# Layer 0 of a fused two-layer transformer: two pairs embedded together, every step of the pipeline placed anew

## What is computed

```python
x0 = concat([cls, patches(x) @ w_tok + b]) + pos        # 37 rows of 256 per image
h  = concat([x0, txt])                                  # 32 sequences of 69 rows of 256
xn = layernorm(h);  A = causal softmax(Q K / 4)         # 16 heads of 16
h  = h + (sum over heads of A V) @ WO + 16*bO           # heads are summed before WO
x2 = layernorm(h);  expert = argmax(softmax(x2 @ Wr))   # 8 experts, one per token
h  = h + max_prob * (relu(x2 @ W1[e]) @ W2[e])
# layer 1: attention with 16 heads, then a ternary-weight feed-forward net with a convolution
```

## Time and profile before

| | us |
|---|---|
| median of 3 runs | 916.31 (915.96 to 918.7) |
| the profiled execution's own time | 916.32 |
| its span, first to last instruction | 914.5 |
| TensorE busy | 784.6 (86%) |
| VectorE busy | 600.3 (66%) |
| ScalarE busy | 438.3 (48%) |
| GpSimd busy | 382.4 (42%) |

### The profile page before, as it was taken

How to read it: one execution, slowest core, us unless ns; L and a number is a source line. 1 busy time by engine, 2 the same in 40 slices (tenths; PEclk the granted TensorE clock), 3 DMA queues, 4 the chain that set the end, 5 groups by cost and what they waited for, 6 DMA issues and landing times.

```text
span 914.5 us, 20695 instructions
## 1 busy us (share of the span) xinstructions
PE 784.6 (86%) x7145; PEld 690.6 (76%) x7145; DVE 600.3 (66%) x1444; ACT 438.3 (48%) x1048; POOL 382.4 (42%) x516
## 2 busy tenths in 40 slices
PE   2799999999999987259999399999999999999743
PEld 2799898999898886136766289898888888888532
DVE  0246666666666665542222035899999999999893
ACT  0234444344344442212222156777887778776552
POOL 0234444444444442232221376666656666543100
PEclk9999999999999998579999699999999999999655
DMA  5324831100000023112221100000000000000000
GB/s 149 92 63 192 199 59 47 19 12 8 8 8 8 11 49 107 41 31 70 64 68 43 30 8 14 8 10 18 14 14 15 14 14 18 16 8 8 10 10 12
DMA packets 23981, 36.41 MB, mean 40 GB/s; under 512 B 10037, under 2 KB 21210, under 8 KB 23114
## 3 DMA queue, kind: packets, MB, share of 16 engines
q1 hardware_dynamic: 14474, 26.20, 10.6%
q0 software_dynamic: 5808, 5.63, 2.8%
q10 hardware_dynamic: 3600, 3.28, 1.1%
HBM read 27.21 MB, written 7.88 MB: 38 GB/s over the span
## 4 chain that ended last, share of the span: by engine, by line
PE 42%; DVE 33%; issue 13%; DMA 4%; ACT 4%; POOL 2%; SPq 1%; DVEq 0%; ACTq 0%; POOLq 0%
PE bank_c L1471 5%; PE bank_h L1434 4%; PE bank_b L1462 3%; PE bank_e L1589 3%; DVE stats L902 3%; PE bank_c L1605 2%; PE bank_f L1589 2%; PE bank_d L1605 2%; DVE diff L1110 2%; DVE w L1167 2%; DVE w L1136 2%; DVE rowmax L1102 2%; DVE diff L896 2%; DVE w L1142 2%; DVE zmax L1161 2%
## 5 line engine op out<-in xcount | busy, mean ns | idle before, releaser
L457 POOL TENSOR_TENSOR qbd<-qt,consts_f 128x560 f32<-128x560 f32 x128 | 163.4, 1283 | 196.6 <-PE bank_e L1406 75.5
L465 POOL TENSOR_TENSOR veps<-mv,consts_f 69x2 f32<-69x2 f32 x64 | 12.4, 194 | 141.9 <-DVE mv L906 104.6
L584 ACT ACTIVATE pt<-bank_g 69x448 f32<-69x448 f32 x64 | 34.9, 545 | 70.3 <-PE bank_h L1416 70.3
L1471 PE MATMUL bank_c<-patches,w_tok 128*128 128x74 f32 x384 | 52.4, 292 | 14.9 <-DMA br<-in_br 14.9
L579 ACT ACTIVATE prob<-diff 112x345 f32<-112x345 f32 x64 | 31.4, 491 | 65.4 <-DVE diff L896 65.4
L1471 PEld LDWEIGHTS bank_c<-patches,w_tok 128*128 128x128 f32 x384 | 50.2, 209 | 14.9 <-issue 14.9
L735 ACT ACTIVATE w<-w,conv 128x138 f32<-128x138 f32 x128 | 54.8, 492 | 9.4 <-DVE w L1119 9.4
L503 POOL DMA_INDIRECT diff<-expert_rows,tile_tokens x25 | 25.1, 1004 | 80.4 <-PE bank_a L1581 54.4
L1780 PE MATMUL bank_b<-f,w 128*69 128x256 bf16 x256 | 37.4, 309 | 15.4 <-ACT w L748 14.5
L484 POOL DMA_INDIRECT expert_lists<-token_no,slot_i x32 | 38.5, 1202 | 22.1 <-issue 14.6
L1434 PE MATMUL bank_h<-values,pt 69*69 69x68 f32 x512 | 39.3, 232 | 8.9 <-ACT pt L584 6.8
(11 more groups left out here) (239 smaller groups left out, 2335.4 us busy)
## 6 DMA issues: line engine op xcount, KB each, us to landing
w<-in_w SPq DMA_DIRECT2D x2, 4096.0 KB, 16.3
patches<-in_patches SPq DMA_DIRECT2D x16, 222.0 KB, 2.7
expert_results<-prob ACTq DMA_DIRECT2D x25, 128.0 KB, 1.9
expert_rows<-x SPq DMA_DIRECT2D x16, 138.0 KB
out<-h SPq DMA_DIRECT2D x16, 138.0 KB
f_raw<-in_f SPq DMA_DIRECT2D x2, 1024.0 KB, 8.5
patches<-in_b SPq DMA_DIRECT2D x1, 2048.0 KB, 10.8
wqkv<-in_wqkv SPq DMA_DIRECT2D x2, 768.0 KB
```

What stands on the lines that cost most here:

```text
L457: pool.tensor_tensor(qbd[u % 2][:], q.broadcast_to([128, NG, HPB, QG]), head_mask.unsqueeze(1).unsqueeze(3).broadcast_to([128, NG, HPB, QG ...
L1471: ins = mm(banks["c"][:, m * 2 * IMG:(m + 1) * 2 * IMG], w_tok[:, c, m * 128:(m + 1) * 128], patch_v[:, bass.ds(s, 1), c, :].rearrange("p ...
```

## The change

Two pairs are embedded by one set of products: `embed(i)` makes half i % 2 of the double pair i // 2 with 148 columns, once per step, where before two halves of 74 columns were made per step. `et` has two buffers, the transposes (`turn_embedded`) are still one pair at a time. The first two pairs' patches are loaded ahead of the attention weights, and the loops of SP are unrolled.

The whole order of layer 0 is replaced on all four engines. Every operation becomes a function of its own (most were already so for layer 1, and those are moved up and shared); the functions `softmax_shift`, `moments`, `attend_out` and `move_pt` are split. The pipeline is deeper: lags reach 6 on TensorE and POOL, 5 on DVE and ACT, where they reached 4.

```diff
-    with sp.Fori(1, PAIRS) as n:
+    load_pair(1)                      # ahead of the attention weights
+    for n in range(2, PAIRS):
...
@@ gpsimd
+            def list_tokens(p):
+                pool.wait_ge(slots_made, p + 1)
+                wait(pool, rows_listed, 32 * p)
+                ... two indirect DMAs as before
             def body(s):
-                spread_queries of pair s-2, units 2 and 3
-                inverse_deviation 1 of s-3
-                the two indirect DMAs of s-4
-                inverse_deviation 0 of s
-                spread_queries of pair s-1, units 0 and 1
+                list_tokens(s - 6)
+                deviation2(s - 4)
+                deviation1(s - 1)
+                spread_query(s - 2, 0), (s - 2, 1), (s - 2, 2), (s - 2, 3)
@@ scalar
             def body(s):
+                exp_scores(s-4, 0), exp_scores(s-4, 1), move_pt_g(s-4, 0), move_pt_h(s-4, 0)
+                move_pt_h(s-4, 1), exp_scores(s-4, 2), move_pt_g(s-4, 1), norm2_routed(s-5)
+                move_pt_g(s-4, 2), move_pt_h(s-4, 2), move_x2(s-5), exp_scores(s-4, 3)
+                move_q(s-3), move_pt_g(s-4, 3), move_pt_h(s-4, 3), move_k(s-3)
+                norm1(s-2), move_embedded(s), move_xt(s-2), move_ot(s-4)
@@ vector
             def body(s):
-                softmax_shift(s-2, 0), (s-2, 1), add and moments of s-3, take_slots(s-4)
-                softmax_shift(s-2, 2), add_base and moments of s, softmax_shift(s-2, 3)
-                attend_out(s-2, 0), choose(s-3), attend_out(s-2, 1), move_v(s-1)
+                shift_scores(s-3, 2), row_max(s-3, 3), add_base(s-1), take_slots(s-5)
+                stats_embedded(s-1), shift_scores(s-3, 3), variance1(s-1)
+                row_sums(s-3, 0), norm_heads_summed(s-3, 0), choose(s-4), sum_heads(s-3, 0)
+                row_sums(s-3, 1), norm_heads_summed(s-3, 1), sum_heads(s-3, 1)
+                row_max(s-2, 0), shift_scores(s-2, 0), move_v(s-2)
+                row_max(s-2, 1), shift_scores(s-2, 1), row_max(s-2, 2)
+                add_projected_heads(s-3), stats2(s-3), variance2(s-3)
@@ tensor
+            def embed(i):
+                d, m = i // 2, i % 2
+                pe.wait_ge(patches_in, 16 * (2 * d + 2))
+                bank_is_free("c", "embed", i)
+                for c in range(FC):
+                    ins = mm(banks["c"][:, 0:4 * IMG], w_tok[:, c, m * 128:(m + 1) * 128],
+                             patch_v[:, 2 * d:2 * d + 2, c, :], start=c == 0, stop=c == FC - 1)
             def body(s):
+                scores(s-4, 3), turn_embedded(s-2), turn_p(s-4, 1), rank(s-6), queries(s-3)
+                attend(s-4, 0), turn_p(s-4, 2), attend(s-4, 1), turn_x2(s-5), attend(s-4, 2)
+                logits(s-5), turn_p(s-4, 3), values(s-3), keys(s-3), attend(s-4, 3), embed(s)
+                scores(s-3, 0), turn_x(s-2), scores(s-3, 1), turn_sums(s-4), scores(s-3, 2)
+                project_sums(s-4), turn_p(s-3, 0)
-            steps(pe, PAIRS, LAGS, body)
+            steps(pe, PAIRS, 6, body)
...
```

More of the change, by code:

```diff
@@ L687, in _ @@
+            steps(act, PAIRS, 5, body)
             act.wait_ge(ffn_w_in, 32)
@@ new lines, in bank_is_free, with bank_is_moved, turn_x, queries @@
+            def bank_is_free(bank, stage, p):
+                wait(pe, BK[bank], read_before(order, bank, stage, p))
+            def bank_is_moved(bank, stage, p):
+                pe.wait_ge(BK[bank], read_after(order, bank, stage, p))
+            def turn_x(p):
+                pe.wait_ge(S["x_made"], 2 * p + 2)
+                bank_is_free("a", "turn_x", p)
+                turn_rows("a", xn).then_inc(S["x_turned"], 1)
+            def queries(p):
+                bank_is_moved("a", "turn_x", p)
+                bank_is_free("c", "q", p)
+                query_or_key("c", 0).then_inc(S["q_made"], 1)
@@ new lines, in keys, with query_or_key @@
+            def keys(p):
+                bank_is_moved("a", "turn_x", p)
+                bank_is_free("a", "k", p)
+                query_or_key("a", 1).then_inc(S["k_made"], 1)
+            def query_or_key(bank, kind):
+                for m in range(KC):
+                    for c in range(KC):
+                        ins = mm(banks[bank][:, m * 2 * TP:(m + 1) * 2 * TP],
+                                 wqkv[:, c, kind * D + m * 128:kind * D + (m + 1) * 128],
+                                 xt[:, c, :, :].rearrange("p b t -> p (b t)"), start=c == 0, stop=c == KC - 1)
+                return ins
@@ L1395, in scores, with values @@
+            def values(p):
+                bank_is_moved("a", "turn_x", p)
+                bank_is_free("b", "v", p)
+                for b in range(2):
+                    for c in range(KC):
+                        ins = mm(banks["b"][0:T, b * D:(b + 1) * D], xt[:, c, b, 0:T], wqkv[:, c, 2 * D:3 * D],
+                                 start=c == 0, stop=c == KC - 1)
+                ins.then_inc(S["v_made"], 1)
+            def scores(p, u):
                 b, m, bank = u // 2, u % 2, "ef"[u % 2]
@@ L1396, in scores @@
                 pe.wait_ge(S["qbd_made"], UNITS * p + u + 1)
[L1397 to L1401 removed]
+                bank_is_moved("a", "k", p)
+                bank_is_free(bank, f"scores{u}", p)
                 sc = banks[bank][0:SR, :]
@@ new lines, in body @@
+                if live(s, 6, PAIRS):
+                    rank(s - 6)
+                if live(s, 3, PAIRS):
+                    queries(s - 3)
+                if live(s, 4, PAIRS):
+                    attend(s - 4, 0)
+                    turn_p(s - 4, 2)
+                    attend(s - 4, 1)
+                if live(s, 5, PAIRS):
+                    turn_x2(s - 5)
+                if live(s, 4, PAIRS):
+                    attend(s - 4, 2)
+                if live(s, 5, PAIRS):
+                    logits(s - 5)
@@ L1484, in body @@
+                if live(s, 4, PAIRS):
+                    turn_p(s - 4, 3)
+                if live(s, 3, PAIRS):
+                    values(s - 3)
+                    keys(s - 3)
+                if live(s, 4, PAIRS):
+                    attend(s - 4, 3)
                 if live(s, 0, PAIRS):
-                    embed(s, 0)
+                    embed(s)
+                if live(s, 3, PAIRS):
+                    scores(s - 3, 0)
                 if live(s, 2, PAIRS):
-                    scores(S, BK, order, s, s - 2, 1)
+                    turn_x(s - 2)
```

660 lines of the change are left out of this document (263 added, 397 removed).

## The result

The changed kernel takes 890.3 us, the median of four runs (885.9 to 894.16), beside 916.13 for the kernel before (914.09 to 918.7): a ratio of 0.9715, with 0.9658 to 0.9772 as its 95% interval. The profiled execution is the one of 892.59 us, span 890.8, so 23.7 us less than the 914.5 of before.

A forecast was written before the change was run, and what follows sets the result against it. Layer 0 was taken as bound by TensorE's own work. The steps (-8.4 us), the start (+1) and the end (-1) summed to -8.4 us on 916.32, so 908 us, with a range of 892 to 922.

The forecast's parts named there:

- 15 steps: Layer 0 from the first scores of pair 0 to those of pair 15: 296.4 us against 304.8, 8.4 less.
- projection to the last scatter landed: Layer 0 behind pair 15's projection: statistics and scatters of pairs 14 and 15 as before, so no change.
- What bounds it: Layer 0 is bound by TensorE's own work; its three waits for ACT make 1.14 us of a 20.59 us step.
- the saving of the embedding: On TensorE, 12 instructions at 148 columns, 1.54 us, replace two halves, 2.68 us: 1.14 us saved a step.
- the floor of a step: TensorE's step without its three waits for ACT and with the embedding's saving: 20.59 - 1.14 - 1.14 = 18.3 us.
- The wait for the scatter: DVE's cast to slot_i waits for the previous pair's scatters; this loop of 13.9 + L makes steps of 20.4 us.
- the landing L of the second scatter: Time from the second scatter's start until it has landed: taken as 6.5 us, bounds 6.2 and 7.8.
- the wait is hidden: Rival: the second scatter lands within 4.4 us, steps are 18.3 us, 879 us in all; chance 12 in 100.
- The start: Ahead of pair 0's first scores: an extra pair loaded and more embedding, so 1 us later, -1 to +3.
- The end: Pair 15's first scores to its projection, 20.8 us before: 1 us less, -3 to +1.
- the slower side: Rival: a longer landing, 0.1 us of it costing 1.1 us; 922 us at 7.8; above 7.1, 20 in 100.
- The third rival: DVE late at the exponential of units 0 or 1: 2 to 5 us in all; others, 4 in 100.

The follow-up runs named there:

- run 1: The changed kernel with two slot_i buffers used in turn, so a pair's cast waits for the scatters of the pair before the last: 870.11 us, ratio 0.9497.
- run 6: The changed kernel with POOL's two scatters moved from the head of its step to behind the second layer norm's deviation: 990.46 us, ratio 1.0787.
- run 5: The kernel before, with SP issuing each pair's store of x2 about 9 us later, away from the second scatter: 916.53 us, one run.
- run 4: The kernel before with the double embedding alone (two pairs embedded together), all orders old: 903.53 us.
- run 3: The changed kernel with each pair embedded by itself, so the new orders alone: 902.72 us.
- run 2: The changed kernel with one slot_i buffer, POOL issuing the scatters one pair earlier, between its second and third spread: 875.26 us.
- run 8: The version of run 1 in which POOL too no longer waits for one pair's scatters to land before issuing the next pair's: 868.13 us, ratio 0.946.
- run 7: The changed kernel with the store of x2 held back some 13 us, to 1.7 us ahead of the second scatter: 911.68 us, ratio 0.9917.

## Why the prediction was wrong, step by step

The sum by its own terms, on the profiled executions:

| term | predicted | measured |
|---|---|---|
| start, to the first scores of pair 0 | +1 | -3.3 (40.04 to 36.74) |
| 15 steps | -8.4 (304.8 to 296.4) | -19.7 (to 285.1) |
| first scores of pair 15 to its projection | -1 | -2.7 (20.8 to 18.1) |
| projection to the last scatter landed | 0 | +1.4 (23.9 to 25.3) |
| experts and layer 1 | 0 | +0.6 |
| sum | -8.4 | -23.7 |

*What bounds it; the saving of the embedding; the floor of a step.* Right. 12 instructions at 148 columns took 1.56 us (predicted 1.54), and TensorE's own step is 18.29 us (18.3), shown by run 1. The first three steps, which have no wait, took 52.83 us (52.8).

*The wait for the scatter.* The place and the loop were right, and run 1, which takes away only this wait, and run 6, which lengthens it, show it. **The failed step is a size in it, the landing L of the second scatter: I took 6.5 us, and it is 5.3 in the typical step.** A smaller one went the same way: the pause of POOL ahead of the first scatter was 0.20 us, not the 0.66 of the earlier trace rows. Of the 1.7 us by which the typical step is shorter than the 20.4 that I put, L is 1.15 and the pause 0.46. The other links were within 0.25 us: the loop is 13.4 + L. At 13.4 + 5.3 = 18.7 us the wait is nearly hidden: of the 2.2 us for which DVE stood at the cast in this step, 0.34 reached TensorE. In the changed kernel the store follows the second scatter by 3.8 us (197.31 and 201.09), as I had worked out. The 6.5 came from the end of layer 0, "the one with no other transfer around it", and was supported by the 7.8 of the steady state and the median of 6.2. All steady rows of the old order carried the store; run 5 shows that without it the same scatters land in 4.0 to 5.5 us. I had named the store as what made 7.8 out of the rest and noted that the new order moves it away, and still let the rows with the store bound L from below. The last scatter of all takes 6.46 to 6.57 us in before, in the changed kernel and in run 1 alike, so it is not a measure of the steady ones; why, stays open.

The middle eight steps took 153.3 us instead of 163.2, the first waited one 22.70 instead of 23.7 (L there 7.50, not 9.8), the last three 56.3 instead of 56.7. Part of the gain from the shorter L was given back in each of these three through a cost that the forecast didn't have, the clock:

```profile
160.00:164.00 4.00, 2.92 (x47) 2.83 (x45) 1.02 (x4) 1.09 (x3) 0.00 (x0) 0.97 0.71 99
164.00:168.00 4.00, 3.18 (x11) 2.23 (x12) 3.76 (x13) 1.72 (x5) 3.37 (x6) 0.50 0.02 6
168.00:173.40 5.40, 5.40 (x40) 4.93 (x39) 1.76 (x5) 1.62 (x4) 0.00 (x0) 0.76 0.01 3
```

These are the windows around a landing of 7.0 us. TensorE had waited 1.99 us for its next weights before 164.82, and then ran at 0.50, the lower level of 1.2 GHz, so that the step took 23.16 us, where 13.4 + 7.0 = 20.4 would have been the loop's. The waits of 2.65 us before 104.80, 0.82 before 296.23 and 1.52 before 315.98 did the same; the one of 1.30 before 144.47 did not. An estimate of what it cost: in the 15 steps TensorE worked for 16 us at the lower level, which costs 8 us, and waited for 9 us; together that is nearly the 17.7 us by which run 1, with neither, is shorter (267.4 against 285.1). So the half clock was about as dear as the waits themselves. Why L was as long as 7.0 and 6.9 us in two of these steps isn't shown; in both, SP issued its store and a load some 4 us behind the scatter. The clock also fits the spread of the runs, 8 us for the changed kernel against 1.3 for run 1, where TensorE doesn't wait: the slower runs have the lower mean clock (0.918 at 892.59 and 894.16, 0.927 and 0.925 at 885.9 and 888.0). That the spread comes from this was only argued.

The Trainium skill, "DMA: Bandwidth & Descriptors", section "Anatomy of one DMA", gives such a DMA about 2.0 us of fixed time. With 1.2 us for the instruction that made 3.2, and the rival "the wait is hidden". No second scatter was that short (3.6 us is the least in any trace here), but the first one of a pair takes 3.8 in nearly all steps, some 2.6 from the end of its instruction. For the second scatter, on which the sum hangs, the 3.2 us are 2.1 us too short in the typical step, where my 6.5 were 1.2 too long; for the first of a pair the page comes nearer, within 0.6 us.

*The start.* Wrong in sign, 4.3 of the 15.3 us by which the sum was off. The extra pair ahead of the attention weights cost less than the estimated 1.5 us: the first product starts at 14.72 us, before at 14.94. In the seven runs that also load this pair first it starts at 15.2 to 16.3, in run 5, which doesn't, at 15.03. The larger part is what stands on the chain, and at which clock. Before, 24 of the instructions ran between `turn_x` of pair 0 and what it led to, as the chain of the start shows, at 215 ns each, where the steady step has 112 (here the chain of the kernel before, then that of the changed one):

```profile
28.44 5.15 PE bank_c L1471 x24
```

```profile
34.44 0.95 PE bank_a L1417 x8
35.40 1.51 PE bank_c L1476 x12
```

Now 12 do, at 126 ns each: 3.6 us less on the chain. The prediction called the slow rate half clock. The profile's column has 1.00 for that stretch (28.20 to 33.60 us), but this isn't a measurement: the trace has no record of the clock there (the first one starts at 36.79 us in the kernel before, at 23.79 in the changed one), and the column counts a stretch without a record as full. Where there is a record, the rate goes with it. In run 4, 12 products of 148 columns take 256 ns each from 31.88 us and 135 ns each from 24.58 us (the columns are those of the earlier trace rows):

```profile
31.88:34.80 2.92, 2.92 (x14) 2.92 (x14) 0.00 (x0) 0.40 (x1) 0.00 (x0) 0.50 0.35 100
24.64:26.20 1.56, 1.56 (x13) 1.53 (x14) 0.00 (x0) 0.00 (x0) 0.00 (x0) 1.00 0.04 12
```

The first 24 products of the changed kernel, ahead of its first record, take 259 ns each, 3.3 us for 12 (6.6 us for both halves, where I put 6.1). So half clock fits what is recorded. By an estimate from these rates, half of the 3.6 us comes from 12 products in place of 24 (5.15 to 3.3) and half from the clock, which my sum left as it was (3.3 to 1.5). Neither half of the change brings the gain alone: the first scores start at 42.72 us in run 3 and at 40.54 in run 4. What lets the clock rise earlier in some kernels, these runs don't show. I had counted instructions that "lie under the wait" without following which stood on the chain of before.

*The end* gave 1.7 us more than I put, within its range of -3 to +1. The term behind the projection came out 1.4 us worse, with L of 8.96 and 6.57 us where it was 7.71 and 6.50.

*The rivals.* The mechanism of the "hidden" one, 879 us, is nearer to the result than the forecast. It failed only by 0.4 us in the typical step and by the few long landings. Landings of 7.0 us and more, the slower side, did happen in two single steps (7.50 and 7.00), and run 6 shows that it would have cost more than the 1.1 us for 0.1 us of L that I put, because of the clock. The third rival had waits at the exponentials of units 0 and 1; the six waits of TensorE for an exponential from 60 to 290 us all stand before `turn_p` of unit 3.

## What to carry to other kernels

A duration of a transfer read in the old order includes its neighbours of the old order: before it goes into the sum of a new order, look for an instance without the neighbour that the change moves away, and if the trace has none, keep the lower bound open. Where an engine that sets the time waits behind a buffer of a few bytes, a second one costs a few lines; here it is worth 20 us on top of the change, where the new orders alone brought 13 to 14. A wait of some us on TensorE is dearer than its length, since the work behind it may run at half clock; here that happened behind waits of less than 1 us too.

## What the runs showed of the hardware that I had not expected

The landing of one small indirect scatter (69 numbers), from the start of its instruction, ranges from 3.0 to 16.8 us over all traces. In the steady steps of run 1, with the store 3.8 us away, the first of a pair takes 3.8 us, the second, issued 1.54 us behind, 3.6 to 6.2. The same pair often has nearly the same value in the changed kernel and in runs 1, 2, 3 and 8 (the eighth 3.6 to 3.8, the third 5.8 to 6.5), so the numbers written, or their places, may matter. They don't decide it alone: the eighth takes 5.5 us in run 5, and the fourth 7.0 in the changed kernel and 4.5 to 5.0 in the four others. No run tested it. A 138 KB store issued 0.3 us behind the second adds about 2 us, one issued 1.7 us ahead nothing in the median of the steady steps (5.3 us in both, from the fifth pair on); the 16.8 was beside 4 MB of weights.

TensorE's granted clock fell to half around single waits of 1.5 to 12.0 us in a stream that was otherwise dense, and the next 3 to 6 us of work ran at it. It also fell behind short ones: 0.82 us before 296.23 in the changed kernel (0.58 over 296.23 to 300.3 us), 0.77 us before 156.93 in run 3, 0.87 us before 222.52 in run 7 (0.61 over 222 to 226 us). Yet one of 1.30 us in the changed kernel, and those of 1.26 and 1.28 us before 53.46 and 329.78 in the kernel before, were followed by none. The length of the wait alone doesn't decide it.
